# Transposing the second expert's rows ahead of the first expert's products, and one shared product instead of two ahead of the last logits

## What is computed

```python
x = x + _wkv(time_decay, time_first, _layernorm(x), ctx_2048)
h = _rmsnorm(_layernorm(x), norm_w)
logits = h @ gate_w.T                     # 32 experts
scores = softmax(logits); topk_w, topk_ids = top_k(scores, 4)
buf[sorted_eid, pos] = h[tok]             # up to 256 rows for each expert
gu = buf @ w13                            # 256 -> 2 * 128
act = silu(gu[:128]) * gu[128:]
eo = act @ w2                             # 128 -> 256
routed[tok] += eo[sorted_eid, pos] * weight
shared = silu(h @ shared_gate_w) * (h @ shared_up_w) @ shared_down_w
out = x + _layernorm(x) + routed + shared
```

## Time and profile before

| what | us |
|---|---|
| median of 3 runs | 169.73 |
| the three runs | 169.05, 169.73, 199.37 |
| profiled execution, own time | 168.31 |
| its span in the profile | 166.6 |
| PE busy | 133.3 (80%) |
| DVE busy | 119.5 (72%) |
| ACT busy | 91.0 (55%) |
| POOL busy | 84.4 (51%) |

### The profile page before, as it was taken

The page is one execution under the profiler, slowest core; times in us unless marked ns, Lnnn a source line. Parts: engine busy times, 40 slices in busy tenths (PEclk is TensorE's granted clock), DMA queues, the critical chain, the costliest instruction groups (busy, mean ns, idle before and its releaser), DMA issues.

```text
span 166.6 us, 2867 instructions
## 1 busy us (share of the span) xinstructions
PE 133.3 (80%) x740; PEld 112.4 (67%) x740; DVE 119.5 (72%) x423; ACT 91.0 (55%) x262; POOL 84.4 (51%) x104
## 2 busy tenths in 40 slices
PE   0235696976979579765979999999999999999691
PEld 0222485765767468544968997997998989888450
DVE  1489999999999864354797778777767688634471
ACT  3632794864853862313566889787774687300011
POOL 8100003675675666670157767777765667772000
PEclk9999999999999999999999999999999999999999
DMA  4999999999999932277999999999674341185987
GB/s 129 292 374 420 420 413 417 374 375 372 370 378 368 363 107 104 97 219 209 336 323 293 362 380 338 371 369 295 193 234 148 100 148 56 49 305 174 342 296 252
DMA packets 32433, 46.49 MB, mean 279 GB/s; under 512 B 3017, under 2 KB 27285, under 8 KB 32156
## 3 DMA queue, kind: packets, MB, share of 16 engines
q1 hardware_dynamic: 27936, 37.15, 65.7%
q0 software_dynamic: 3888, 8.53, 14.2%
q10 hardware_dynamic: 588, 0.54, 1.0%
HBM read 27.95 MB, written 20.48 MB: 291 GB/s over the span
## 4 chain that ended last, share of the span: by engine, by line
PE 41%; DVE 29%; DMA 12%; issue 8%; ACT 5%; POOL 2%; SPq 1%; ACTq 0%; POOLq 0%; DVEq 0%
PE bank L1051 19%; PE bank L1068 11%; DVE S L635 6%; PE bank L1037 5%; DMA w_all<-rows_out 5%; DVE ND L648 3%; DMA rows_in<-n_row,slot_all 2%; DMA rows_out<-w_all,pick_idx 2%; PE bank L1115 2%; DVE R L665 2%; DVE DR L658 2%; DMA xg<-rows_in 2%; PE bank L994 2%; DVE ekv L629 1%; DMA rows<-in_L_ffn_norm_w_dram 1%
## 5 line engine op out<-in xcount | busy, mean ns | idle before, releaser
L380 POOL DMA_INDIRECT rows_out<-w_all,pick_idx x49 | 48.3, 985 | 28.1 <-DVE w_all L872 9.4
L366 POOL DMA_INDIRECT rows_in<-n_row,slot_all x32 | 31.9, 998 | 37.8 <-DVE slot_all L732 30.2
L1051 PE MATMUL bank<-xT,w_all 128*128 128x128 f32 (+2 forms) x256 | 40.9, 303 | 1.7 <-ACT xT L535 0.7
L1051 PEld LDWEIGHTS bank<-xT,w_all 128*128 128x128 f32 x256 | 35.6, 191 | 4.2 <-issue 3.6
L535 ACT ACTIVATE xT<-bank,nws 128x256 f32<-128x256 f32 x64 | 26.9, 471 | 15.6 <-PE bank L1037 15.3
L1068 PE MATMUL bank<-w_all,act_t 128*128 128x256 f32 x92 | 25.3, 382 | 1.1 <-DVE act_t L866 1.1
L866 DVE TENSOR_TENSOR act_t<-sg,bank 128x256 f32<-128x256 f32 x32 | 13.4, 418 | 14.0 <-ACT sg L540 13.9
L1068 PEld LDWEIGHTS bank<-w_all,act_t 128*128 128x128 f32 x92 | 15.6, 191 | 2.5 <-issue 1.8
L1037 PE MATMUL bank<-ident,xg 128*128 128x128 f32 x92 | 15.5, 274 | 1.8 <-DMA xg<-rows_in 1.8
L540 ACT ACTIVATE sg<-bank 128x256 f32<-128x256 f32 x32 | 12.3, 383 | 8.6 <-PE bank L1051 7.9
L1037 PEld LDWEIGHTS bank<-ident,xg 128*128 128x128 f32 x92 | 11.7, 141 | 5.6 <-issue 2.9
(11 more groups left out here) (142 smaller groups left out, 230.1 us busy)
## 6 DMA issues: line engine op xcount, KB each, us to landing
w_all<-in_L_ffn_w_dram SPq DMA_DIRECT2D x12, 1024.0 KB, 14.3
rows_in<-w_all SPq DMA_DIRECT2D x8, 1056.0 KB, 12.4
xg<-rows_in SPq DMA_DIRECT2D x32, 264.0 KB, 5.2
w_all<-rows_out SPq DMA_DIRECT2D x2, 1024.0 KB, 5.1
w_all<-rows_out SPq DMA_DIRECT2D x2, 512.0 KB, 7.3
w_all<-rows_out SPq DMA_DIRECT2D x4, 256.0 KB, 7.9
rows_out<-w_all,pick_idx POOLq DMA_INDIRECT x49, 2.8
x_all<-in_x_dram SPq DMA_DIRECT2D x1, 768.0 KB, 5.3
```

The source lines that it names most:

```text
L366: pool.indirect_dma_start(rows_in, bass.IndirectOffsetOnAxis(ap=slot_all[:, b, k:k + 1], axis=0), n_row[:, b, :], None)\
L380: pool.indirect_dma_start(rows_out, bass.IndirectOffsetOnAxis(ap=pick_idx[:, e, a:a + 1], axis=0), yo[e][:, a, :], None, bounds_check=PICK ...
L1051: last = nc.tensor.matmul(FG[j][:, a, lo:lo + slots], w13_all[:, expert(e), h, a, :], xT[:, j, h, lo:lo + slots], start=(h == 0), stop=(h ...
```

## The change

Two edits. On PE and ACT the steps of experts 0 and 1 are regrouped: both are transposed and copied first, then both have their gate and up products, then both silus follow; from expert 2 on the order is as it was. And in the last tile's `logits` one product of the shared expert stands ahead of the logits' matmuls where two did; the second goes to where `positions` had the third, and the later ones move up by one, so that all four products of the second pair of tiles come behind the totals (`TOT`, L1007).

```diff
@@ scalar engine
             rows_to_sbuf(0, 0)
-            for e in range(E):
-                if e == 0:
-                    silu(0, 0)
+            rows_to_sbuf(1, 1)
+            silu(0, 0)
+            silu(1, 1)
+            for e in range(1, E):
                 if e < E - 1:
                     rows_to_sbuf(e + 1, (e + 1) % 2)
                 if e > 2 and e % 2:
                     free_rows(e // 2 - 1)
-                if e:
+                if e > 1:
                     silu(e, e % 2)
@@ tensor engine, logits and positions of the last tile
                 if b == B - 1:
                     pe.wait_ge(s["base_ready"], B - 1)
                     pe.wait_ge(s["sh_in"], 32)
-                    for h in range(HC):
-                        shared_part(0, 0, h)
+                    shared_part(0, 0, 0)
...
                 if b == B - 1:
-                    shared_part(0, 1, 0)
+                    shared_part(0, 0, 1)
@@ behind the pipeline
+            shared_part(0, 1, 0)
+            pe.wait_ge(s["base_ready"], B)
             shared_part(0, 1, 1)
-            pe.wait_ge(s["base_ready"], B)
-            shared_part(1, 0, 0)
             pe.wait_ge(s["picked_done"], B)
             pe.wait_ge(s["earlier_done"], B)
...
-            for h in range(1, HC):
+            for h in range(HC):
                 shared_part(1, 0, h)
@@ experts
             rows_to_channels(0, 0, second(0))
             shared_down(1)
-            for e in range(E + 1):
-                if e == 0:
-                    gate_up(0, 0, second(0), third(0))
+            rows_to_channels(1, 1, second(1))
+            gate_up(0, 0, second(0), third(0))
+            gate_up(1, 1, second(1), third(1))
+            for e in range(1, E + 1):
                 if e + 1 < E:
                     rows_to_channels(e + 1, (e + 1) % 2, second(e + 1))
                 if e == 1:
                     pe.wait_ge(s["slot_max_done"], 1)
                     nc.tensor.transpose(TOPT, slot_max[:, :], ident[:, :]).then_inc(s["topT_ready"], 1)
-                if 0 < e < E:
+                if 1 < e < E:
                     gate_up(e, e % 2, second(e), third(e))
-                if e:
-                    down(e - 1, (e - 1) % 2, second(e - 1))
+                down(e - 1, (e - 1) % 2, second(e - 1))
```

## The result

| | before | after |
|---|---|---|
| median of 20 executions each, same chip | 169.12 us | 167.14 us |
| profiled execution: own time | 168.31 us | 166.68 us |
| its span | 166.6 us | 164.9 us |
| last tile's logits begin | 63.38 | 62.70 |
| expert 0's products begin | 75.69 | 75.60 |

The ratio is 0.9895, with a 95% interval of 0.9873 to 0.9917: about 1.8 us of 169.1 less. Ratios and intervals here are formed from executions within 1.5% of the fastest of their kernel, and need not equal the quotient of the two medians beside them. The forecast was 0.95 us less and 168.0 us; 167.14 lies in the range of 166.7 to 169.7, near its lower end.

The account below looks back on a forecast made before the run. The path through logits, scatters and expert loads, then DVE up to `gated(3)`, then busy PE was taken as the bound. 0.1 + 0.85 = 0.95 us off the 169.0 mean gave 168.0 us, range 166.7 to 169.7.

Parts of the forecast that it names:

- Part one, the logits: Last tile: with one shared product fewer ahead, the logits wait for `hT` and begin 0.65 us earlier (0.85 upper end).
- POOL's wait: POOL's wait for the last row numbers, ahead of its scatter: about 0.9 us expected, not 1.56.
- PE's slack ahead of expert 0's transposes: PE was free at 72.62, expert 0's rows now come at about 72.4; moved work uses this up and costs nothing.
- Part two, the new wait: `gate_up(0)` stands behind expert 1's rows (3.9 us load): expert 0's products begin at 75.6, 0.1 us earlier, not 0.65.
- The rival that the new wait eats the gain: At `gate_up(0)`: expert 1's load beyond 3.9 us costs one for one, no gain from 4.85; 168.8 to 169.5; chance 0.22.
- Part two, the wait removed: `gate_up(1)` no longer stands behind expert 2's rows, so `gated(1)` follows the picks without 0.85 us of waiting.
- From `gated(1)` to PE's restart, one for one: DVE has no wait from `gated(1)` to `gated(3)`, so PE's restart at 87.04 and the end move by the same 0.95 us.
- The sum, 0.95: At `gated(1)`: 0.1 us from expert 0's earlier products plus 0.85 us from the removed wait, 0.95 us in all.
- The rival of the clock: PE in 70 to 80 us: added idling ahead of the logits delays the clock's rise; net 2 us slower, 171; chance 0.06.
- More than the sum (167.4), 0.15: Expert 1's load takes under 3 us, so 1.6 us are gained and the time is 167.4 us; chance 0.15.

Follow-up runs that it names:

- series 1: Follow-up runs on one chip, kernel before at 168.68 us: each edit alone, no product ahead of the logits, expert 0's products ahead of expert 1's transposes.
- series 4: Follow-up runs on one chip, kernel before at 169.30 us: changed kernel with weight ordering moved to expert 5, and regrouping alone with five unread products.
- regrouping with the added products: Kernel before with only the regrouping, plus five unread shared products where PE idles: 187.66 and 186.97 us on slow chips, 167.39 us (ratio 0.9895) on a fast one.
- series 2 and 3: Follow-up runs on chips with a longer second stage; the kernel before takes 187.88 and 187.77 us there.
- expert 0 first: Changed kernel with expert 0's gate and up products ahead of expert 1's transposes, and its silu ahead of expert 1's copies: 168.69 us, ratio 0.9987.
- the weights later: Changed kernel with DVE's ordering of the weights moved from expert 2 to expert 5: 186.65 and 186.24 us on slow chips, 166.83 us (ratio 0.9891) on a fast one.

## Why the prediction was right, step by step

**Part one, the logits (0.65 earlier): right.** In the changed kernel they begin 0.68 earlier, and with that edit alone 0.79 earlier, 0.57 to 0.62 of which arrive from the scatter on (the logits' row is 0.16 longer behind a wait). That `hT` takes over as the bound is shown by the kernel without any product in front: the same start, 0.71 us of waiting. POOL's wait came out at 0.95 for about 0.9 foreseen. PE's slack ahead of expert 0's transposes did absorb the moved work (they began at 72.91, 72.8 foreseen).

**Part two, the new wait (expert 0's products at 75.6): right,** 75.60, with 3.8 us for expert 1's load. The match to 0.1 us has luck in it: in the profiles of series 1 and 4 that load took 3.3 to 4.2 us. The remark among the rivals that those products "could have begun earlier without it" was true and of no worth: the kernel that does so begins them 0.32 earlier and ends 1.5 us later. The rival that the new wait eats the gain looked at that wait alone. The experiment shows what the wait buys: expert 1's copies lie beside it instead of behind expert 0's silu.

**Part two, the wait removed (0.85): right.** `gated(1)` at 79.66 with no wait (79.7 foreseen), `down(0)` at 78.31 (78.1). The regrouping alone shows the same at its own times: `gated(1)` at 81.00 without a wait, in spite of the clock.

**From `gated(1)` to PE's restart, one for one: short by 0.18.** 1.02 became 1.20. Of this, 0.12 come because the copy of `down(0)`'s result no longer waits for its matmuls; the rest, 0.06, is the two instructions L835 behind `gated(2)`, 0.35 us where they took 0.41, for which no cause is shown. The prediction had `down(0)` two us early and did not ask what DVE had waited for before. That DVE bounds this piece is shown by moving its weight ordering away: `gated(3)` came 0.57 earlier against `gated(1)`. The prediction took from this that an early us arrives at the end. With that kernel it was not seen to (0.6 of 0.8 gone again, in one profile of each), with the logits edit it was (about 0.5 of 0.6, by the times).

**The sum, 0.95: too small, about 1.8 (1.4 to 2.1 by the interval).** The range of 166.7 to 169.7 held the time, but it holds the 169.12 of the kernel before as well, so that it did says little for the mechanism. The terms of the sum were about right in size; what is missing lies outside it:

- 0.18 us on DVE, above.
- About 0.25 us for TensorE's clock. Nine of 29 executions of the kernel before had a low clock and were 169.39 - 168.57 = 0.82 us slower; 9/29 x 0.82 = 0.25. On the chip of series 4 it was six of eleven, which would give 0.45. None of the changed kernel's 20 was low; the clock of the executions that it was compared with is on record for one only (1.000). That the low clock of the kernel before falls in the same stretch is inferred from the regrouped kernel's profile and from the equal means. No profile of the kernel before caught it; the one with a third product ahead of the logits, on another chip, did.
- The rest, about 0.4 us, is open. Without the executions of low clock, the kernel without a product in front, whose order is otherwise that of the change, stands 1.26 us below the kernel before (167.31 against 168.57); 0.95 + 0.18 leaves only 0.13 of that. From PE's restart to the end of the span it took 79.1 us in the changed kernel's profile, 79.6 in that kernel's, and 79.3 to 79.9 in the other profiles of series 1 and 4. So the 0.4 us behind the restart in the two profiles compared here are no more than what executions with the same work there differ by.

How the gain divides between the two edits is not shown, since the times do not add. Without low clock, the logits edit alone gives 0.53 us and the regrouping alone 1.25 (three executions), but both together, without a product in front, 1.26 (six). The regrouping with the added products stands 1.37 below the kernel before (167.47, six, against 168.84, five), although its profiled execution restarts PE only 0.23 us earlier (86.81 against 87.04); that execution, 167.93, is the slowest of the six. The positions in the profiles bear out the sum for each part, and the times give the regrouping more.

**The rival of the clock: the mechanism exists, the sign and the place were wrong.** The prediction put the danger in the changed kernel, by 0.2 us of idle time more, and had a late rise in mind. The record of the clock begins with the high level at 68.1 in the changed kernel, and at 68.7 before. What costs in some executions is a fall behind the rise, at 74.2 in the profile of series 1 that caught it, and there the rise itself was late, 70.8. On the chips of series 1 and 4 the low means belong to the kernel before and, more often, to the regrouping alone (two of twelve with the logits edit alone); in the changed kernel and the three others with both edits none of 44 executions was. In series 2 and 3 the profiles of two kernels with both edits have the fall too, so it is not gone everywhere. Its price in series 1 and 4 was 0.8 to 1.1 us, not the net 2 of the rival.

Busy time in a fixed stretch does not say when: PE was busy 4.16 of 6.00 us in 68 to 74 ahead of the fall, but up to 70.8 at half speed; it was 3.87 in the changed kernel and 3.37 in the kernel before, whose clocks stayed up. Of the profiles without added products, those whose clock rose by 68.7 had no fall near 74 to 82 us, and of the six that rose at 69.8 or later four had one (not that with expert 0 first, 70.0, nor that with the weights later in series 2, 76.1). With the five added products none of three had it, at 69.4, 70.9 and 71.5. What sets the rise, and what decides on the fall, is not known.

The Trainium skill (TensorE: Matmul & The Clock Gate, "HAM oscillation — how this bites in real kernels") says that waits between short pieces of PE work bring the array back to half rate, and that the next piece then runs slow. The prediction set this aside because the products at 73 to 80 us had the short spacing in the one profile at hand. The profile of the regrouped kernel agrees in kind, 0.57 in 74 to 78 us, and one profile without a fall was no evidence against the rule. It does not happen every time: three of that kernel's twelve executions had no low mean.

**More than the sum (167.4), 0.15:** nearest to the time, for the wrong reason and so by luck. Its mechanism, a load of under 3 us, did not happen (3.8).

## What to carry to other kernels

Where an engine waits anyway, put the next unit's fetch, transpose and copy into that wait, even if this gives the first unit's products a second thing to wait for: what counts is the first engine that then has no wait at all, here DVE at `gated(1)`. Ask of every step that comes early what the consumer had waited for before: the copy's wait of 0.12 us has no bracket in its row. And take the granted clock from many executions, not from one profile: a fall that comes in a third of them costs a few tenths on average. Here, on one chip, it came more often with the regrouping alone and in none of 18 executions with both edits, and on another five idle-time products kept it away. Last, compare on several chips: on two of the four chips of the experiments the place of part one was not on the path in any profile.

## What the hardware showed unexpectedly

**The clock dip in some executions only.** By its mean clock, the regrouped kernel kept the high level from the rise to nearly the end in three of twelve executions and lost it for a while in nine; in the one that was profiled, from 74.2 to 77.6 us. For the first stage the windows of the kernel before read full speed (1.00 in 30 to 60 us). Those of the regrouping with added products, in series 4, read this:

```profile
30.00:60.00 30.00, 23.60 (x128) 19.79 (x127) 27.64 (x95) 18.88 (x64) 19.23 (x19) 0.50 1.03 359
```

PE's busy time is 23.60 us there and 23.50 in the kernel before, for the same 127 or 128 instructions. So both ran that stage at 1.2 GHz, and the clock row of the kernel before was wrong ahead of its first record at 68.7 us. The spacing of the matmuls says so without the row, as the prediction read it.

**The same program on another chip at 187.8 us.** On two of the four chips of the experiments the executions of every kernel took 183.5 to 192.6 us. Most of the difference lies in the second stage: from the sixth expert's products to the last's it took 67 to 71 us, where the others need 54.4 to 55.0. The timeline of the kernel with the weights later in series 2 shows waits of this kind, that the same kernel does not have in series 4:

```profile
93.24 0.42 DVE L867 TENSOR_TENSOR act_t<-sg,bank 128x256 f32<-128x256 f32 x1 [2.80 <-issue]
93.83 1.12 PE L1068 MATMUL bank<-w_all,act_t 128*128 128x256 f32 x4 [1.60 <-issue]
...
126.60 0.42 DVE L867 TENSOR_TENSOR act_t<-sg,bank 128x256 f32<-128x256 f32 x1 [3.58 <-issue]
```

They are marked as issue, time in which the engine waited for nothing that the profile shows. What the engines waited for is open. The intervals there are 0.009 to 0.015 wide, in series 1 0.006 to 0.008.
